# State-space and output stages of a two-layer model in one block

## The reference

```python
proj = xn @ in_proj_w.T                      # gate 8192 | x, B, C 8192 + 2*8*128 | dt 128
xBC = silu(conv(xBC) + conv_b)               # 4 taps along the tokens
y = ssd(x, A, B, C, D, dt)                   # 128 heads of 64, 8 groups of 16 heads
g = y * silu(gate)
g = (g_by_group * rsqrt(mean(g_by_group**2) + eps)) * norm_w     # 8 groups of 1024 channels
x = x + g @ out_w.T + (xn @ W.T + bias) + lora_B @ (coef * (lora_A @ xn))
```

## Time and profile before

| | |
|---|---|
| median of 3 runs | 2173.74 us |
| profiled execution, its own time | 2171.02 us |
| its span | 2169.3 us |
| TensorE busy | 2094.6 us (97%) |
| VectorE, ScalarE, POOL busy | 68%, 61%, 40% |
| last pass, from step 8 | 1717.8 to 1772.0 us |
| seam to the first gated tile | 1772.0 to 1800.9 us |
| 64 gated tiles | 1800.9 to 2161.0 us |

### The profile page before, as it was taken

The page is one execution under the profiler, slowest core; times in us unless marked ns, Lnnn a source line. Parts: engine busy times, 40 slices in busy tenths (PEclk is TensorE's granted clock), DMA queues, the critical chain, the costliest instruction groups (busy, mean ns, idle before and its releaser), DMA issues. The chain is left out here.

```text
span 2169.3 us, 34257 instructions
## 1 busy us (share of the span) xinstructions
PE 2094.6 (97%) x12040; PEld 1553.2 (72%) x12040; DVE 1466.7 (68%) x1813; ACT 1331.7 (61%) x2368; POOL 866.2 (40%) x758
## 2 busy tenths in 40 slices
PE   6999999998999999999999999999999979999998
PEld 4644444576777777777777777777777747888886
DVE  4466666385478778878687787788787755555555
ACT  2255555534587888788787878788787753323222
POOL 1011111130266666657576666667576660000000
PEclk9999999999999999999999999999999989999999
DMA  3422222231455545555455555554455547444462
GB/s 134 178 78 75 74 75 65 78 136 56 120 162 167 167 137 173 159 166 162 145 171 160 150 163 161 158 175 153 152 168 162 164 163 268 145 134 142 140 216 75
DMA packets 184019, 310.44 MB, mean 143 GB/s; under 512 B 20512, under 2 KB 96800, under 8 KB 183744
## 3 DMA queue, kind: packets, MB, share of 16 engines
q1 hardware_dynamic: 183872, 308.53, 45.4%
HBM read 252.52 MB, written 55.68 MB: 142 GB/s over the span
## 5 line engine op out<-in xcount | busy, mean ns | idle before, releaser
L145 PE MATMUL ssm_pp<-xhi,ssm_lo 128*128 128x512 f32 x1192 | 480.1, 403 | 4.1 <-DVE ssm_bc L1577 3.4
L147 PE MATMUL ssm_pp<-xhi,ssm_hi 128*128 128x512 f32 x1192 | 466.4, 391 | 0.0
L146 PE MATMUL ssm_pp<-xlo,ssm_hi 128*128 128x512 f32 x1192 | 465.9, 391 | 0.0
L1476 ACT ACTIVATE ssm_sct<-ssm_cumb,ssm_gpar 128x128 f32<-128x128 f32 x1024 | 313.1, 390 | 70.8 <-DMA ssm_cumb<-dt_sums 43.9
L137 POOL TENSOR_TENSOR ssm_lo<-ssm_raw,ssm_hi 128x512 fp32r<-128x512 f32 x149 | 243.6, 1640 | 91.6 <-ACT ssm_hi L126 91.6
L145 PEld LDWEIGHTS ssm_pp<-xhi,ssm_lo 128*128 128x128 f32 x1192 | 224.2, 188 | 67.3 <-issue 19.1
L1577 DVE SCALAR_TENSOR_TENSOR ssm_xc<-ssm_pp,vectors,ssm_xc 128x1022 f32<-128x1022 f32 (+2 forms) x192 | 245.2, 1277 | 34.7 <-ACT ssm_xc L1435 30.0
L147 PEld LDWEIGHTS ssm_pp<-xhi,ssm_hi 128*128 128x128 f32 x1192 | 224.3, 188 | 48.0
L146 PEld LDWEIGHTS ssm_pp<-xlo,ssm_hi 128*128 128x128 f32 x1192 | 224.7, 188 | 42.6
L1612 DVE TENSOR_TENSOR ssm_sct<-ssm_sct,ssm_cbm 128x1024 f32<-128x1024 f32 x128 | 228.5, 1785 | 27.9 <-ACT ssm_sct L1483 27.9
L1744 POOL TENSOR_TENSOR ssm_go<-ssm_t,ssm_gt 128x512 f32<-128x512 f32 x128 | 165.1, 1290 | 168.7 <-DVE ssm_t L1648 168.7
(11 more groups left out here) (224 smaller groups left out, 3970.3 us busy)
## 6 DMA issues: line engine op xcount, KB each, us to landing
ssm_cumb<-dt_sums SPq DMA_DIRECT2D x96, 1024.0 KB, 5.9
ssm_raw<-w SPq DMA_DIRECT2D x149, 256.0 KB, 5.5
gated<-ssm_go SPq DMA_DIRECT2D x128, 256.0 KB, 4.4
out_graw<-gated SPq DMA_DIRECT2D x64, 512.0 KB, 4.0
out_raw<-w SPq DMA_DIRECT2D x65, 256.0 KB, 2.6
ssm_cumb<-dt_sums SPq DMA_DIRECT2D x32, 512.0 KB, 3.9
ffn_raw<-w SPq DMA_DIRECT2D x37, 256.0 KB, 2.7
stk_qs<-qk_parts SPq DMA_DIRECT2D x96, 64.0 KB, 2.2
```

The lines of the kernel that those rows point to most:

```text
L145: pe.matmul(out, wlo, xhi, start=start, stop=False)
L146: pe.matmul(out, whi, xlo, start=False, stop=False)
L147: return pe.matmul(out, whi, xhi, start=False, stop=stop)
L1476: i = act.activation(sct[:, s % 2, h, :], cumb[:, s % 2, 0, h, :], ACT.Relu, scale=-1.0, bias=gpar[:, unit, 0, s % NTOK, h:h + 1])
```

## The change

Both stages become one program block. What it does:

1. Weight tiles are reordered: W 0 to 2, lora_A, W 3, lora_B. So base tiles 0, 1, 2 and 4 are W, tile 3 is h, and lora_B is split by the state-space feed as one tile more, in steps 12 and 13.
2. Base tiles stay on chip. The first two go to the homes of B and C, two to unit 0 of x. h is not copied; its halves are made from PSUM (`lora_high` in step 14, `lora_low` in step 15).
3. rstd of groups 0 to 6 is made two steps earlier. In step 14 SyncE loads the first weight and gated tiles, in step 15 rstd of group 0.
4. The output stage uses tiles that are idle in the last pass: gt, xc, sct, xhi, xlo, cumb, the feed's ring. Its 8 PSUM banks are those of the state-space stage, and h's products enter bank by bank as these come free.
5. All 64 gated tiles are written out, with no hardware loop.
6. At the end VectorE takes each output tile when its banks are done. The last tile is taken in two halves.
7. The 29 semaphores are cleared by POOL at the start of the state-space block.

```diff
-            return not (last and isinstance(r[0], int) and r[0] >= G) or r[1] < NPRE
+            return not (last and isinstance(r[0], int) and r[0] >= G) or r[1] <= NPRE
...
-        def pre_dst(i):
-            return xc[:, 0, i, :] if i < CU else gt[:, 0, 0, :]
+        base = (bc[:, 0, :], bc[:, 1, :], xc[:, 0, 2, :], xc[:, 0, 3, :])
...
+        o.raw, o.gs = wide(gt[:, 0, 0:2, :]), gt[:, 0, 2:4, :]
+        o.graw = (xc[:, 0, 0, :], xc[:, 0, 1, :], flat(sct[:, 0, :, :]), flat(sct[:, 1, :, :]))
+        o.hi, o.lo = wide(xhi[:, 0:2, :]), wide(xhi[:, 2:4, :])
+        o.g_hi, o.g_lo = xlo[:, 0:2, :], xlo[:, 2:4, :]
...
-                    if last and s >= HALF_AT + 2 and (s - HALF_AT) % 2 == 0:
-                        base_out((s - HALF_AT) // 2 - 1)
...
+                        squares_out(G - 1, 0)
+                    if last and s == 14:
+                        out.first_loads(sp)
+                    if last and s == 15:
+                        out.first_rstd(sp)
...
             def copy_pre(i):
                 act.wait_ge(tile_done, G * GT + (i + 1))
-                act.wait_ge(t2_done, G * NS - NTOK)
-                act.wait_ge(g_done, G * NS - NTOK)
-                act.activation(pre_dst(i), slot(i), ACT.Copy).then_inc(pre_done, 1)
+                k = i if i < LORA else i - 1
+                if k < 2:
+                    act.wait_ge(c_copied, G)
+                    act.wait_ge(cb_sum, G)
+                    act.wait_ge(bt_turned, G)
+                else:
+                    act.wait_ge(t2_done, G * NS - NTOK)
+                act.activation(base[k], slot(i), ACT.Copy).then_inc(pre_done, 1)
...
+    def first_loads(self, sp):
+        self.o.unit0_gated(sp)
+        self.load_w(sp, 0)
+        self.o.groups_written(sp, G - 1)
+        self.o.unit0_summed(sp)
+        self.load_g(sp, 0)
+        self.load_w(sp, 1)
+        self.load_g(sp, 1)
...
+    def sync(self, sp, squares_out):
+        o.scores_read(sp)
+        o.unit1_summed(sp)
+        o.unit1_gated(sp)
+        for n in range(G * NB):
+            g, j = divmod(n, NB)
+            if n >= 2:
+                self.load_w(sp, n)
+            if n + 2 == (G - 1) * NB:
+                o.groups_written(sp, G)
+            if n + 2 < G * NB:
+                self.load_g(sp, n + 2)
+            if g == 0 and j < G - 2:
+                sp.dma_start(o.rs[j + 1], c.rs_dram[j + 1].partition_broadcast(P)).then_inc(m.rest_in, 16)
+            if n == 1:
+                squares_out()
+            if n == 2:
+                o.squares_written(sp)
+                for unit in range(2):
+                    sp.dma_start(self.halves[:, unit, :], over_partitions(c.var_dram[unit, G - 1:G])
+                                 ).then_inc(m.sq_in, 16)
...
+    def tensor(self, pe, last_squares):
+        o.weights_split(pe)
+        pe.wait_ge(m.lora_lo, B)
+        o.base_copied(pe)
+        for bank in range(4):
+            lora(bank)
+        o.turn_read(pe)
+        lora(7)
+        o.unit1_summed(pe, 1)
+        lora(4)
+        o.unit1_summed(pe)
+        lora(5)
+        last_squares()
+        for n in range(G * NB):
+            pe.wait_ge(m.g_lo_done, n + 1)
+            pe.wait_ge(feed.lo_done, n + 1)
+            if n == 0:
+                for bank in (0, 2, 4, 1, 3, 5, 7):
+                    gated(n, bank)
+                o.squares_copied(pe)
+                lora(SQ)
+                gated(n, SQ).then_inc(m.tile_done, 1)
+            elif n < G * NB - 1:
+                for bank in (0, 2, 4, 6, 1, 3, 5, 7):
+                    mm = gated(n, bank)
+                mm.then_inc(m.tile_done, 1)
+            else:
+                for bank in range(8):
+                    mm = gated(n, bank, True)
+                    if bank in (1, 3, 5, 6, 7):
+                        mm.then_inc(m.sums_done, 1)
...
+    def vector(self, dve):
+        scale_g(0)
+        low(0)
+        for n in range(G * NB):
+            if n == 3:
+                dve.wait_ge(m.sq_in, 32)
...
+            if n + 1 < G * NB:
+                scale_g(n + 1)
+            g_low(n)
+            if n > 0:
+                low(n)
+        dve.wait_ge(m.base_added, KT)
+        for n, (k, bank, cols) in enumerate(o.pairs):
+            dve.wait_ge(m.sums_done, n + 1)
+            dve.scalar_tensor_tensor(o.x[:, k, cols], bank, c.vec[:, V_OB + k:V_OB + k + 1], o.x[:, k, cols],
+                                     ALU.add, ALU.add).then_inc(m.added, 1)
```

More of the change, by code:

```diff
@@ L78, in after, with __init__ @@
         eng.wait_ge(sem, value)
+class FeedMarks:
+    def __init__(self, nc, ctx, name, raw_slots):
+        self.arrived = [ctx.enter_context(nc.semaphore(f"{name}_arrived{s}")) for s in range(raw_slots)]
+        self.hi_done = ctx.enter_context(nc.semaphore(f"{name}_hi_done"))
+        self.lo_done = ctx.enter_context(nc.semaphore(f"{name}_lo_done"))
 class Feed:
-    def __init__(self, nc, ctx, name, slots, raw_slots, used, side="left", home=None):
+    def __init__(self, nc, ctx, name, slots, raw_slots, used, side="left", home=None, marks=None, halves=None):
         self.slots, self.raw_slots, self.used = slots, raw_slots, used
@@ L1165, in passes, with groups_written @@
+        def groups_written(eng, groups):
+            for q in g_out:
+                eng.wait_ge(q, groups * (NS // 2) * 16)
+        o.groups_written = groups_written
+        out = Output(nc, ctx, c, w, marks, o, x_out)
+        block = ctx.enter_context(nc.Block())
         def passes(eng, body):
@@ L1189, in parameters, with write @@
                              ).then_inc(dec_in[unit], 16)
-            def out(g, s):
+            def write(g, s):
                 sp.wait_ge(g_done, g * NS + (s + 1))
@@ L1413, in body, with last_squares @@
                         turn(g + 1, 0)
+            def last_squares():
+                pe.wait_ge(sqs_done, G * NS)
+                pe.wait_ge(var_done, G * 2 - 1)
+                squares(1)
             passes(pe, body)
-            pe.wait_ge(sqs_done, G * NS)
-            pe.wait_ge(var_done, G * 2 - 1)
-            squares(1)
+            out.tensor(pe, last_squares)
         @block.scalar
@@ L1545, in body @@
                         square(*before(g, s, 2))
-                    if last and s == 13:
+                    if last and s == 11:
                         act.wait_ge(rms_sum, 1)
@@ L1688, in body @@
                         finish(*before(g, s, 1))
-                    if last and s == 12:
+                    if last and s == 10:
                         dve.wait_ge(rms_in, 32)
@@ new lines, in __init__ @@
+        (self.tile_done, self.sq_in, self.eps_set, self.std, self.rstd, self.rstd_out, self.rstd_in, self.x_in,
+         self.scaled, self.g_hi_done, self.g_lo_done, self.added, self.stored, self.sq_sum,
+         self.base_added, self.rest_in, self.sums_done, self.lora_hi, self.lora_lo) = several = [sem(n) for n in (
+            "tile_done sq_in eps_set std rstd rstd_out rstd_in x_in scaled g_hi_done g_lo_done added stored "
+            "sq_sum base_added rest_in sums_done lora_hi lora_lo").split()]
```

384 lines of the change are left out of this document (178 added, 206 removed).

## The result

| | before | after |
|---|---|---|
| median | 2173.55 us (2171.22 to 2174.24) | 2137.09 us (2136.12 to 2137.97) |
| span of the profiled execution | 2169.3 us | 2134.4 us |
| TensorE busy | 2094.6 us | 2080.5 us |

The ratio is 0.9834, with a 95% interval of 0.9817 to 0.9851: faster, by 1.7%. Besides the idle time that was to go, TensorE's own busy time fell by 14.1 us. For 11.5 of them, those of the gated tiles, the forecast had no term.

A forecast was written before the change was run, and what follows sets the result against it. TensorE, busy for 97% of the span, was taken to bound the kernel, so only its idle or slow-clock time could be won. 17.2 + 4.5 - 1.0 + 3.7 = 24.4 us gave a median of 2149, range 2141 to 2160.

The forecast's parts named there:

- Part 1, the seam: From the last y product's end into the gated tiles: 28.9 us becomes 11.7, gain 17.2 (13.5 to 20.0).
- The 1.3 us for the clock: In the seam: half of the half clock's 2.7 us price, after 2.7 us idle; bounds 0 and 2.7.
- Part 2, the copies: Last state-space pass: base copies to B and C homes gain 4.5 us; lora_B's extra split and low half lose 1.0.
- The long form of the low half: Last pass: POOL's extra low half, contending with VectorE, would make the sum about 1 us worse.
- Part 4, the steady output stage: Gated tiles: same products and bank order, operands in other homes, loop written out at no cost; 0 us.
- pace: Rival, 0.12 in all: homes or order change product pace by 1.5%; quicker gives 2144, or 2138 with weight savings (0.06).
- Part 5, the tail: Behind the last product: VectorE takes finished bank pairs early; 4.1 us plus about 0.5 against 8.3, gain 3.7.
- Part 3, base tiles on chip: Base tiles' writes and reads dropped; the 2 MB read lay beside a saturated TensorE, so worth nothing.
- Supply: Rival, chance 0.13: SyncE's single queue delays loads over the first four gated tiles, losing 5 to 12 us; 2154 to 2162.
- No change: Rival, chance 0.05: saved idle time returns as POOL and rstd waits, under 4 us left; 2170 to 2178.
- slower: Case, chance 0.06: new homes or instruction fetching slow each gated tile; at 10% it would give 2185.

The follow-up runs named there:

- y3: Kernel before with the first two base copies of the last pass going to the B and C homes, writes to memory kept; 2168.8 us, ratio 0.999.
- y4: Kernel after with rstd of group 0 loaded first in step 14 and lora_B's low half made by VectorE; 2135.03 us, ratio 0.984.
- x4: Kernel before with only its end changed: last tile bank by bank, VectorE taking each output tile when its banks are done; 2167.77 us, ratio 0.998.
- x3: Kernel after with 32 unused bytes between xhi and xlo; 2162.7 us, ratio 0.9953.
- z4: Kernel after run once more without any edit; 2137.11 us, ratio 0.9838.
- x2: Kernel after with 32 unused bytes ahead of both xhi and xlo, shifting both operands together; 2134.21 us, ratio 0.9822.
- z3: Kernel after with 256 unused bytes between xhi and xlo; 2138.98 us, ratio 0.9847.
- y1: Kernel before with 96 unused bytes ahead of the output stage's rstd tile; 2160.92 us, ratio 0.995.
- y2: Kernel before with 224 unused bytes ahead of the output stage's rstd tile; 2167.39 us, ratio 0.9984.
- x1: Kernel before with 32 unused bytes ahead of the output stage's rstd tile; 2170.98 us, ratio 0.9998.
- z1: Kernel after with y4's edits, gated tile 0's low half made earlier, and the squares behind three of its banks; 2135.29 us, ratio 0.9829.

## Why the prediction was wrong, step by step

**Part 1, the seam: right.** Said 17.2 us, with 13.5 to 20.0 as bounds; it was 18.7. The first gated tile was forecast at T0 + 9.7 and came at 9.6; rstd was to land after 5.0 us and took 4.8. Two readings in it were off without moving the sum much. The squares came at T0 + 6.8 and not 6, since VectorE's scaling slowed POOL's last sum. And the prediction lists the clock's falls as behind the waits of 3.52 and 11.71 us; the granted clock of before had already fallen at 1776.9, inside the wait of 5.89 us, and stayed at the half to 1797.3:

```profile
1776.90:1797.30 20.40, 7.64 (x18) 4.69 (x19) 3.27 (x5) 3.32 (x4) 0.92 (x2) 0.50 0.53 186
```

That is why the squares took 1.92 us there and 1.05 after. The 1.3 us for the clock was a mean of two outcomes. The profiled execution had neither a drop nor the price, the other four paid 1.4 to 2.8. So the closeness of 17.2 to 18.7 is in part luck: with the clock lost the seam gains 15.9 to 17.2. This is a term that one trace can't settle: it belongs in the range, not in the middle.

The Trainium skill's section that the prediction names for the fixed cost of a transfer ("DMA: Bandwidth & Descriptors", anatomy of one DMA) is on transfers that POOL issues. Those of this kernel are SyncE's, and what counts for them is the row of 2.5 us for 256 KB. The Trainium skill gave no term of the sum.

**Part 2, the copies: right.** Said 4.5 less 1.0; y3 shows 4.0 for the copies. For lora_B's low half y4 shows 0.7 to 1.1 (it moves the load of rstd as well), and the kernel after is 1.3 behind y3 in the pass. The mechanism is the one named, and y3 has the gain with the writes to memory in place. The long form of the low half didn't come: it took 1.27 us at 1755.70, and VectorE ran nothing with two SBUF inputs beside it.

**Part 4, the steady output stage: this step failed.** It read "The looped and the written-out stretches of before have the same pace ..., so writing it out costs nothing". That is true of the loop and says nothing of the homes, since both stretches use the same ones. "Each operand pair in other homes" was listed and priced at 0. It was worth 11.5 us, and with it the sum would have been 24.4 + 11.5 = 35.9 and the median 2138.

The *pace* rival had it, and gave it 0.06. It was also mis-sized: it took 391 to 397 ns as 1.5% of 360 us, 5.4 us. But these durations overlap, products start 234 ns apart. A difference of 6 ns, if it is one of pace, counts for each of 1536 products with its full 6 ns, which is 9.2 us and a median near 2140. That the rival also names 2138, 1 us from the result, is luck: it gets there by a saving on weights that no run shows. Read from the starts, the state-space products of the same trace (227 ns in the median) against those of the output stage (234.3 ns) would have given about 7.5 ns and 11 to 12 us. The reading was open in the trace of before; what couldn't be known from it is whether the new homes would be of the quick kind.

**Part 5, the tail: right.** Said 3.7, it was 3.9, and x4 shows 3.9 alone. **Part 3, base tiles on chip: right at 0**, as far as y3 tells it, where the writes are still made.

**Supply** didn't happen: no wait on TensorE from tile 1 on, though SyncE's queue is in the order that was feared. The halves landed after 4.4 us and not 7.1, at about T0 + 17.5. **No change** and **slower** didn't happen either. That homes can cost time was a sound suspicion, though: x3 shows that 32 bytes more between two tiles would have taken back 25.6 of the 36.5 us.

**What stays open.** That the distance modulo 256 sets the pace in a long run of such products is shown, at six distances (0 in many homes; 32, 128, 160, 192 and 224 slow, at means of 231 to 235 ns). Why isn't. One story is that the read of the moving tile meets that of the next weights, since a weight load runs beside each product. It is only argued: no run had products without a load beside them. In this simple form it doesn't fit x3 either: beside its products of xlo the trace has the load of ssm_hi, which is at distance 0 from xlo too, and still the next product starts 231.5 ns later and not 227.

Nor does the rule hold in every stage. In the attention stage products of xhi with ffn_hi lie, at distance 0, in short groups between products of other shapes. Followed by another product of this stage, they have a median pace of 231 to 233 ns in the kernel after, z4, x2 and z3, and of 227 in x3, where the distance is 224. What counts there was not looked for.

## What to carry to other kernels

Measure TensorE's pace from start to start in every stage of a kernel that is "100% busy", and compare stages: a stage that needs 234 ns where another of the same shape needs 227 may have 3% to give, and unused bytes may fetch them. For long runs of products with a weight load each, keep small tiles out from between the large ones, or round them up, so that moving tiles and weights start at the same place modulo 256 bytes. When a change moves operands to other homes, cost the homes as a part of its own, and try it by itself with a few unused bytes.

## What the runs showed of the hardware

The relative start of TensorE's two operands in SBUF changes its pace in the output stage, at a granted clock of 1.00: 226.7 ns per product of 128x512 with a weight load each at distance 0 modulo 256 bytes (after, y1, z3), 232.4 at 128 (y2), 233.3 at 32 (x3) and 192 (x1), 234.3 at 160 (before). It isn't a rule for every stage, as the attention stage shows. The Trainium skill ("TensorE: Matmul & The Clock Gate", the step-by-step part on what happens when a matmul is issued) says that loading the next weights takes no SBUF read bandwidth from the running product, and gives 215.7 ns from start to start at full clock. No stretch here ran at that figure: the quick ones are at 226.7 ns, and here the measurement decides. Whether the load is what costs the rest isn't shown, so what the Trainium skill says of the load is neither borne out nor refuted; that the start addresses of the two operands count is shown.

TensorE's granted clock after a wait can't be told from the wait's length: behind 1.8 and 1.8 us it was kept in one execution and lost in four, behind 3.5 us kept in y2 and lost in the kernel before, x1, x4 and y1.

POOL's small additions took 0.73 us or, in y4 and z1 beside VectorE's scaling, 1.71 for the same form, and moving VectorE's work earlier cost the chain that it was to help.
